# Who issues the stores of the padded tiles: ScalarE's queue in place of SyncE's, and the order of SyncE's gathers

## The reference, cut to what matters

```python
x = x + _L0_conv_ref(_gn(x), ...)   # a selective scan over the 1024 pixels (Mamba), its projections and layer norms
x = x + _L1_conv_ref(_gn(x), ...)   # linear attention with a 5x5 convolution
```

```python
qkv = jnp.einsum('bchw,oc->bohw', x, qkv_w)                    # 256 -> 768 channels
agg = conv_general_dilated(qkv, dw_w, (1, 1), ((2, 2), (2, 2)), feature_group_count=768)
agg = jnp.einsum('bgihw,goi->bgohw', agg.reshape(B, 96, 8, H, W), pw_w)
q, k, v = relu(t[:, :, :8]), relu(t[:, :, 8:16]), t[:, :, 16:]   # t: qkv and agg, 64 heads in all
vk = jnp.einsum('bhdn,bhen->bhde', v1, k)                      # v1: v with a row of ones
out = jnp.einsum('bhde,bhen->bhdn', vk, q); out = out[:, :, :-1] / (out[:, :, -1:] + 1e-15)
out = jnp.einsum('bchw,oc->bohw', out, proj_w)                 # and the batch norm
```

## Time and profile before

| what | value |
|---|---|
| time, median of 3 runs (lowest, highest) | 665.24 us (664.08, 667.45) |
| the profiled execution: its own time, its span | 671.67 us, 669.9 us |
| PE busy / its weight loads | 618.6 us (92%) / 438.1 us (65%) |
| VectorE / ScalarE / GpSimd busy | 530.5 us (79%) / 381.3 us (57%) / 368.6 us (55%) |
| chain that ended last: PE / DVE / DMA / ACT | 80% / 6% / 6% / 4% of the span |
| of it the stores `patch_rows<-arena` | 5% of the span |
| stores `patch_rows<-arena` | 10 of 648 KB, median 7.5 us to landing |
| gathers `arena<-patch_rows` | 40 of 324 KB, median 6.2 us to landing |

### The profile page before, as it was taken

One profiled execution on the slowest core, in us unless ns is written; L12 is line 12 of the kernel. 1 busy time (PEld: TensorE's weight loads), 2 busy tenths in 40 slices (PEclk: granted clock), 3 DMA queues, 4 the chain that ended last, 5 costly groups with the idle time before them and its releaser, 6 DMA issues.

```text
span 669.9 us, 25303 instructions
## 1 busy us (share of the span) xinstructions
PE 618.6 (92%) x11404; PEld 438.1 (65%) x11404; DVE 530.5 (79%) x546; ACT 381.3 (57%) x743; POOL 368.6 (55%) x164
## 2 busy tenths in 40 slices
PE   2999999899978999999999999999799699999997
PEld 1443445789967788877888779888655455555533
DVE  5795612899979999998878999996978697992465
ACT  1774785987866777778666777621155345333100
POOL 1000504599988898899988899990400044533000
PEclk9998999999999999999999999999799799999999
DMA  6990645200363201522430100016059899790203
GB/s 224 75 82 6 170 139 170 63 20 20 75 146 88 67 20 41 139 50 83 113 97 20 51 19 21 3 36 196 1 114 187 174 243 211 179 176 0 59 7 125
DMA packets 72626, 62.11 MB, mean 93 GB/s; under 512 B 34024, under 2 KB 57576, under 8 KB 72520
## 3 DMA queue, kind: packets, MB, share of 16 engines
q1 hardware_dynamic: 71560, 60.09, 40.6%
q10 hardware_dynamic: 960, 0.41, 0.2%
HBM read 44.22 MB, written 15.25 MB: 89 GB/s over the span
## 4 chain that ended last, share of the span: by engine, by line
PE 80%; DVE 6%; DMA 6%; ACT 4%; issue 3%; SPq 1%; DVEq 0%; ACTq 0%
PE PS L1119 34%; PE PS L1138 8%; PE PS L1001 7%; PE PS L1253 7%; DMA patch_rows<-arena 5%; PE PS L1344 4%; PE PS L1166 4%; PE PS L1359 4%; PE PS L1135 2%; PE PS L972 1%; PE PS L1232 1%; SPq L483 1%; PE PS L1330 1%; PE PS L1010 1%; PE PS L1028 1%
## 5 line engine op out<-in xcount | busy, mean ns | idle before, releaser
L558 POOL TENSOR_TENSOR X<-X,spare 128x2048 f32<-128x2048 f32 x32 | 146.9, 4590 | 10.0 <-DVE X L1576 8.6
L1119 PE MATMUL PS<-mid,arena 128*32 128x128 f32 x4096 | 133.2, 273 | 8.6 <-issue 7.3
L1119 PE MATMUL PS<-WPR,arena 128*32 128x128 f32 x2048 | 127.5, 273 | 8.1 <-DVE X L1580 2.9
L1119 PEld LDWEIGHTS PS<-mid,arena 128*32 128x32 f32 x4096 | 118.2, 110 | 25.3 <-issue 19.2
L1119 PEld LDWEIGHTS PS<-WPR,arena 128*32 128x32 f32 x2048 | 112.7, 110 | 24.4 <-issue 14.4
L1119 PE MATMUL PS<-APROD,arena 128*32 128x128 f32 x2048 | 126.1, 274 | 1.2 <-issue 0.9
L788 ACT ACTIVATE arena<-arena,small 128x512 f32<-128x512 f32 (+1 forms) x150 | 99.5, 713 | 34.7 <-DVE X L1580 11.5
L1119 PEld LDWEIGHTS PS<-APROD,arena 128*32 128x32 f32 x2048 | 109.7, 110 | 2.7 <-issue 2.4
L583 POOL TENSOR_TENSOR arena<-arena,PWR 128x512 f32<-128x512 f32 x30 | 40.6, 1383 | 72.7 <-PE PS L1253 72.6
L558 POOL TENSOR_TENSOR arena<-arena,spare 128x2048 f32<-128x2048 f32 x16 | 73.3, 4583 | 6.0 <-DVE arena L1576 5.4
L558 POOL TENSOR_TENSOR WIN<-WIN,spare 128x2048 f32<-128x2048 f32 x16 | 73.4, 4586 | 3.7 <-DVE WIN L1576 2.7
(11 more groups left out here) (192 smaller groups left out, 1060.0 us busy)
## 6 DMA issues: line engine op xcount, KB each, us to landing
arena<-dt_rows SPq DMA_DIRECT2D x56, 256.0 KB, 4.1
arena<-patch_rows SPq DMA_DIRECT2D x40, 324.0 KB, 6.2
patch_rows<-arena SPq DMA_DIRECT2D x10, 648.0 KB, 7.5
X<-in_x SPq DMA_DIRECT2D x4, 1024.0 KB, 7.5
dt_rows<-arena SPq DMA_DIRECT2D x8, 512.0 KB, 3.2
spare<-c_rows SPq DMA_DIRECT2D x64, 64.0 KB, 2.2
tap_rows<-WPR SPq DMA_DIRECT2D x24, 88.0 KB, 8.6
mid<-dt_rows SPq DMA_DIRECT2D x8, 256.0 KB, 3.5
```

Of the source, the lines that this page charges most:

```text
L558: pool.tensor_tensor(HB[s % 4], HB[s % 4], CROW[:, k % 2:k % 2 + 1, :].broadcast_to([P, QN, HALF]), ALU.mult).then_inc(S["g_rd"], 1)
L1119: mm = pe.matmul(PS[32 * n:32 * n + 32, 4 + i, j * P:(j + 1) * P], DXT[:, DT_ * b + g, 4 * h + j, 32 * i:32 * i + 32], DIAGB[k % 2][n][:, ...
```

## The change

SyncE's `store_patches` goes away. ScalarE issues the same DMA itself in `take_qkv(k)`, behind the four copies of a tile, after a wait for its own four copies, and ahead of `RAW` or of the rectified copy (whose wait for the same copies it takes over). SyncE keeps the gathers, those of tiles 0, 1 and 3 in a row, then `load_taps(1)`, then those of tile 4, and goes on as before without the stores. The line numbers of the changed kernel are 9 lower behind the removed lines, and 7 lower behind the added ones.

```diff
@@ SyncE
-            def store_patches(k):
-                sp.wait_ge(S["pad_rd"], 4 * k + 4)
-                sp.dma_start(patch_rows[k, 0:P * 8 * AREA].rearrange("(p m) -> p m", p=P), PATCH[slot_of(k)[0]].rearrange("p y x a b -> p (y x a b)")).then_inc(st_patch[slot_of(k)[0]], 16)
...
-            for k in (0, 1, 3, 4, 5, 6):
-                store_patches(k)
-                if MADE[k][0] < 2:
-                    take_patches(k, 0)
-                    take_patches(k, 1)
-                if k == 0:
-                    load_taps(1)
+            for k in (0, 1, 3):
+                take_patches(k, 0)
+                take_patches(k, 1)
+            load_taps(1)
+            take_patches(4, 0)
+            take_patches(4, 1)
             for n in range(2, CONVS):
...
-                if n < 4:
-                    store_patches((7, 10)[n - 2])
                 take_patches(one, 1)
                 take_patches(two, 1)
-                if n < 4:
-                    store_patches((9, 11)[n - 2])
@@ ScalarE, take_qkv(k)
+                act.wait_ge(S["pad_rd"], 4 * k + 4)
+                act.dma_start(patch_rows[k, 0:P * 8 * AREA].rearrange("(p m) -> p m", p=P), to.rearrange("p y x a b -> p (y x a b)")).then_inc(st_patch[slot], 16)
                 if not is_q(n):
...
                 if is_q(n):
-                    act.wait_ge(S["pad_rd"], 4 * k + 4)
```

## The result

The changed kernel takes 661.09 us (median of 8 runs, 658.52 to 663.60) against 665.33 us for the one before (8 runs, 664.08 to 667.45): the ratio is 0.9925, with a 95% interval of 0.990 to 0.995, or 3.3 to 6.7 us less. A second series gave 660.78 against 665.10 us, ratio 0.9928 (0.9901 to 0.9954).

A forecast was written before the change was run, and what follows sets the result against it. It took PE as the bound, but in the early second block four stores in a row of about 8 us each. Gain 7.0 - 0.15 - 0.35 = 6.5 us, 665.24 to 658.7 us, range 656.0 to 664.2.

The forecast's parts named there:

- Where the time was lost before: PE at conv(0): 7.11 us idle for tile 3's gathers plus 2.24 us of lower clock, 9.35 us lost.
- conv(0) at 519.8: PE's conv(0) start, from bytes over two rates (22.5 us of DMA) plus 0.9 us of landing; before 525.46.
- VectorE is late next, take_chunk(0) at 524.30: VectorE goes from its four taps straight to take_chunk(0), at 524.30 in place of 530.61: 6.31 us earlier.
- The rule against the change: Skill page: starting DMAs from several engines saves only issue time; read strictly, 2 to 4 us gained, about 662 us.
- ScalarE's share: ScalarE's added wait, 0.2 us, and store issue, 0.5 us, per tile; mostly hidden, 0.15 us lost at tile 4.
- Rivals 2 and 3: ScalarE's store issues last 2.76 us (664.2 us, chance 0.10); or ScalarE is held until the landing (680, 0.04).
- GpSimd beside the taps: GpSimd's placing of taps now runs beside VectorE's taps that count: 0.35 us lost, the multiplication overlapping as before.
- qkv(9) 6.5 us earlier: PE's qkv(9): 7.0 us gained, less 0.15 at tile 4 and 0.35 for GpSimd's placing.
- So PE now waits 1 us for them: PE, there at 542.0, waits for tile 8's copies, done at 543.24, and starts qkv(9) at 543.3.
- rival 4: PE's clock falls at the new wait before qkv(9), costing 3.3 us: 662.0 us, chance 0.08.
- Rival 5: The wait belongs to the profiled execution, not to the runs; the time stays at 665 us, chance 0.08.
- Rival 1: Stores beside gathers cost 20% more engine time, conv(0) starts about 523.7: 663.2 us, chance 0.11.

The follow-up runs named there:

- e7: The changed kernel with qkv(9) behind conv(4) and ScalarE's copies of tile 8 behind its take_conv(2) and tile 6's second half: 655.77 us, ratio 0.9872 to before.
- e1: The kernel before, stores still in SyncE's queue, each put ahead of the gathers of the tile before it: 657.95 us, ratio 0.9923 to before.
- e9: e1 with both edits of e8 (the reordering of e7 and the GpSimd wait of e3): 657.10 us, ratio 0.9891 to before.
- e8: e7 with, in addition, GpSimd's second multiplication of group 1's weights held back until VectorE's 25th tap: 655.28 us, ratio 0.9864 to before.
- e3: The changed kernel with GpSimd's second multiplication of group 1's weights held back until VectorE's 25th tap: 658.76 us, ratio 0.9923 to before.
- e10: The kernel before with the two edits of e7 (qkv(9) and ScalarE's copies of tile 8 later): 663.43 us, ratio 0.9975 to before.

## Why the prediction was right or wrong

- **Where the time was lost before**: right. The wait for tile 3's gathers and the clock behind it went, and e7 shows that nearly their whole sum, 8.9 of 9.35 us, could be had.
- **conv(0) at 519.8** in the clock of before, 19.6 us behind qkv(3): measured 19.04 and 19.33 in the two profiles of the change. The sum of bytes over the two rates was good to 0.5 us, but some of that is luck. Its condition, "that the engines never run dry", didn't hold: the share was 0.76 and 0.75 from 497 to 499 and 0.18 from 508 to 509, while the round trips of tiles 1 and 3 were awaited. Against that, the engines were full some 0.5 us earlier than the sum had it, and moved up to 417 GB/s with a store among the gathers, where the sum had 351 for a store.
- **VectorE is late next, take_chunk(0) at 524.30**, 24.07 us behind qkv(3): measured 24.04, with no wait. Right.
- **Why a store needs 8 us**: in part wrong. The prediction puts it down to the store's place in SyncE's list. In a list of its own tile 3's store still took 7.66 us, and landed at 513.4 in the clock of before. Of the turns between queues, which the prediction takes from the Trainium skill, page "DMA: Bandwidth & Descriptors", section "Queues, rings and completion order", these rows show little: ScalarE's stores of tiles 1 and 3 moved no packet in the first 2 and 3 us behind their issue, where tile 0's, with nothing else in flight, had 0.33 MB moved 1.6 us behind its own. Then they did get most of the engines, tile 1's 0.58 MB from 493 to 495 against 0.15 of gathers, with 0.52 MB of gathers still moved behind it. (The kernel's first 20 us also have two busy queues in the trace of before, which the prediction overlooked.)
- **The rule against the change**: read strictly, it gave about 662 us, which lies nearer to 661.09 than the forecast does. The number doesn't decide it, the traces do: e1 has the gain without a second queue, as the rule would have it, but by an order of the list and not by issue time, and e9 against e8 leaves the queue some 1.9 us.
- **ScalarE's share**: 0.2 + 0.5 us forecast for wait and issue; the row of RAW at 510.73 stands 0.42 us behind the last copy, with the issue, 0.33, in between. The 0.15 us at tile 4 was 0.05 at VectorE's taps (18.88 against 18.83 us behind qkv(3)). Too high, by little. Rivals 2 and 3 are out: no issue over 0.35 us.
- **GpSimd beside the taps**: 0.35 us forecast, for the placing; measured 0.79 (16.77 against 15.98 us for the eleven taps), of it 0.89 for the last four and 0.10 back at the four before. Some 0.7 of that is the second multiplication (see e3). With that held back, what is left for the placing varied from nothing (15.97 in e8) to 0.5 us (16.46 in e3). The sentence that failed is "the multiplication itself still overlaps as much as before": the second multiplication waits for conv(3), which came earlier than the 25th tap now.
- **qkv(9) 6.5 us earlier**: measured 50.10 - 43.86 = 6.24. Right within 0.3.
- **"So PE now waits 1 us for them"**: measured 2.77, where the forecast's own times, 542.0 and 543.3, make 1.3. conv(0) ended 0.5 us sooner than forecast, so PE was there sooner, and the taps that tile 8's copies wait for took 0.8 us longer. The 19.3 us of work that PE has in between were right (19.2).
- **"I think not"** on the clock at the new wait: this is the term that was missing from the sum, rival 4 with a chance of 0.08 and 3.3 us. I had PE waiting 1 to 3 us there and took the two falls of the earlier trace rows, after 4.8 and 4.95 us, for the least that it takes. It fell after 2.77 and 2.86 us, and cost 1.77 and 3.07. 6.24 - 1.77 leaves 4.5 of the 4.4 us measured.
- **Rival 5**, that the profiled execution had the wait to itself: wrong, the extra time lay ahead of qkv(3), and e10 has the wait without it. Rival 1: conv(0) came 0.2 to 0.5 us earlier than the sum said, though the engines ran partly dry, so no extra cost of stores beside gathers shows.

The range held, and the direction; the point was 2.4 us too low, for the clock.

## What to carry to other kernels

When a DMA that is ready stands in a list behind another buffer's round trip, reorder the list or use another queue; the profile shows it as engine share near zero between two transfers that follow each other. Before counting the gain, follow the engine that becomes late to its next consumer: the waits of 2.8 and 2.9 us there cost PE another 1.8 and 3.1 in clock, and a short filler or another order of the steps (on every engine whose list holds the awaited step) got it back. A helper that starts earlier may now share time with the work that has become critical; here GpSimd's multiplication and VectorE's taps.

## What the runs showed of the hardware

- How long PE may idle before the clock falls can't be read off one profile. Idle stretches of 2.54, 2.77, 2.86, 3.74, 6.70 and 7.11 us were followed by matmuls at the lower level; one of 2.78 us (e9) was not, nor any of the ten between 0.4 and 1.7 us in the table. The fall needn't come in the wait: with the change it came almost a microsecond after PE had started again in one profile, and 0.8 us before that in the other.
- The price of a fall differed between two profiles of one kernel: 1.77 and 3.07 us on the same matmuls. It went with how long the clock stayed at 0.50, some 3.4 and 6.8 us (6.6 in the earlier trace rows). What decides that stays open.
- Two queues at once cost nothing that shows: the half tile that conv(0) waits for landed 0.2 to 0.5 us before the sum of bytes over single-queue rates. But a second queue did not make a store land at once either: with gathers in flight tile 3's took 7.66 us, its first 3 without a packet moved; tile 0's, alone, was through in under 3. ScalarE's issues took 0.33 us each, whatever SyncE had in its queue, where SyncE's own took up to 2.76.
